# Routed expert stage in pairs of tiles, on one Trainium2 core

## The reference, cut to what matters

```python
ys = _geglu(xf @ Ws1 + bs1) @ Ws2 + bs2                    # shared expert
top_val, top_idx = jax.lax.top_k((xf @ Wr + br) / TAU, 2)
w = ...                                                    # softmax of the two, one-hot over 12
h = jnp.einsum('nd,edh->enh', xf, We1) + be1[:, None, :]   # first layer, 256 -> 2 x 768
yE = jnp.einsum('enh,ehd->end', _geglu(h), We2) + be2[:, None, :]
yr = jnp.einsum('end,ne->nd', yE, w)                       # out = ys + yr + residual
```

## Time and profile before

| | us |
|---|---|
| median of 3 runs (824.36 to 825.64) | 825.05 |
| the profiled execution, its own time | 824.58 |
| its span | 822.7 |
| PE busy | 793.7 |
| DVE busy | 571.9 |
| POOL busy | 406.8 |
| ACT busy | 301.0 |

### The profile page before, as it was taken

The page is one execution under the profiler, slowest core; times in us unless marked ns, Lnnn a source line. Parts: engine busy times, 40 slices in busy tenths (PEclk is TensorE's granted clock), DMA queues, the critical chain, the costliest instruction groups (busy, mean ns, idle before and its releaser), DMA issues. The chain is left out here.

```text
span 822.7 us, 27871 instructions
## 1 busy us (share of the span) xinstructions
PE 793.7 (96%) x9379; PEld 663.5 (81%) x9380; DVE 571.9 (70%) x1323; ACT 301.0 (37%) x855; POOL 406.8 (49%) x511
## 2 busy tenths in 40 slices
PE   8989999999999999889999999999999999999994
PEld 7778888888888888657777888888888888888884
DVE  3887777777777779867886666766766666666652
ACT  1434444444444444443332333333333333333330
POOL 3144444444444444200103477777777777777762
PEclk9999999999999999999999999999999999999998
DMA  8634555555555543026853222322322322322222
GB/s 275 209 106 158 172 167 174 175 175 175 173 151 177 171 121 99 2 70 187 267 194 87 80 38 35 39 34 33 39 35 33 39 35 33 41 33 34 40 29 27
DMA packets 49294, 85.61 MB, mean 104 GB/s; under 512 B 7298, under 2 KB 27970, under 8 KB 49122
## 3 DMA queue, kind: packets, MB, share of 16 engines
q1 hardware_dynamic: 33778, 68.83, 26.2%
q0 software_dynamic: 13888, 15.13, 13.8%
q10 hardware_dynamic: 1584, 1.10, 0.5%
HBM read 68.48 MB, written 16.55 MB: 103 GB/s over the span
## 5 line engine op out<-in xcount | busy, mean ns | idle before, releaser
L1515 PE MATMUL ps<-arena,stage 128*128 x900 | 206.6, 379 | 0.0
L1515 PEld LDWEIGHTS ps<-arena,stage 128*128 128x128 f32 x900 | 165.2, 190 | 19.5
L494 POOL DMA_INDIRECT out_dram<-stage,to_row x75 | 120.7, 1609 | 75.0 <-DVE stage L1098 68.2
L674 ACT ACTIVATE stage<-ps 128x384 f32<-128x384 f32 x150 | 65.4, 488 | 241.1 <-PE ps L1502 241.1
L1502 PE MATMUL ps<-token_rows,token_rows_T 64*128 64x128 f32 x1800 | 129.2, 272 | 0.0
L1502 PEld LDWEIGHTS ps<-token_rows,token_rows_T 64*128 64x128 f32 x1800 | 118.8, 188 | 1.7
L486 POOL DMA_INDIRECT token_rows<-gated_rows,from_row x75 | 75.2, 1003 | 63.9 <-DVE to_row L980 41.2
L1072 DVE COPY token_rows<-ps 128x128 f32<-128x128 f32 x75 | 21.8, 291 | 111.6 <-PE ps L1484 111.6
L401 POOL TENSOR_TENSOR arena<-arena 128x256 f32<-128x256 f32 x32 | 23.4, 731 | 153.4 <-DVE arena L797 140.9
L760 DVE TENSOR_REDUCE arena<-ps 128x8 f32<-128x512 f32 x64 | 43.8, 685 | 65.7 <-PE ps L1224 65.1
L1082 DVE TENSOR_TENSOR stage<-ps,stage 128x384 f32<-128x384 f32 x150 | 75.9, 547 | 1.8 <-ACT stage L674 1.8
(11 more groups left out here) (173 smaller groups left out, 1474.3 us busy)
## 6 DMA issues: line engine op xcount, KB each, us to landing
stage<-in_we_dram SPq DMA_DIRECT2D x36, 512.0 KB, 4.4
arena<-in_cond_w_dram SPq DMA_DIRECT2D x64, 256.0 KB
arena<-in_we_dram SPq DMA_DIRECT2D x12, 768.0 KB, 4.8
arena<-in_x_both_dram SPq DMA_DIRECT2D x31, 256.0 KB, 2.6
arena<-in_L_cond_bias_dram SPq DMA_DIRECT2D x64, 64.0 KB, 3.0
out_dram<-arena SPq DMA_DIRECT2D x32, 128.0 KB, 1.7
be_bc<-in_be_rows_dram SPq DMA_DIRECT2D x13, 192.0 KB, 2.8
gated_rows<-token_rows POOLq DMA_DIRECT2D x2, 1152.0 KB, 11.2
```

The costliest lines, as they stand in the source:

```text
L494: pool.indirect_dma_start(out_rows, bass.IndirectOffsetOnAxis(to_row[:, t:t + 1], 0), y_sb[t % YR], None, compute_op=ALU.add).then_inc(d_a ...
L674: nc.scalar.activation(g_sb[hf].rearrange("p (j n) -> p j n", n=P), first_out[1][:, :, hf, :], ACT.Gelu).then_inc(g_ok, 1)
L1515: last = mm(ps[:, 4 + s % 2, 0:D], actT_sb[s % 2][:, hf, j * P:(j + 1) * P], arena[:, ds(e * E2 + (NJ * hf + j) * D, D)], start=(hf == 0 a ...
```

## The change

The routed stage goes in pairs of tiles. Tile 0 goes alone, and then for each odd t PE does first_layer(t), first_layer(t+1), rows_transpose(t+2), rows_transpose(t+3), second_layer(t-2), second_layer(t-1). The first layer gets two PSUM places (banks 0 to 5, two banks of them shared by both places), the second layer writes to bank 6 or 7, and there are three product buffers, the third in the space of `ws2`. ACT copies the bias weights in place of POOL. ACT widens the rows of tiles t+4 and t+5 at the end of pair t, and POOL issues both gathers and both additions of a pair in a row.

The core of the diff, shortened, in the order POOL, ACT, DVE, PE:

```diff
+            def next_rows(t):
+                pool.wait_ge(y_ok, t + 1)
+                if t + RING < NS:
+                    load_rows(t + RING, t % RING)
+            pool.wait_ge(h_ps, 1)
+            copy_last(2)
+            for t in range(1, NS, 2):
+                for n in (t + 2, t + 3):
+                    if n < NS:
+                        pool.wait_ge(h_ps, n - 1)
+                        copy_last(n)
+                if t > 1:
+                    add_rows(t - 2, (t - 2) % RING)
+                    next_rows(t - 2)
+                    next_rows(t - 1)
+                add_rows(t - 1, (t - 1) % RING)
+                if t == 1:
+                    next_rows(0)
...
+            def gelus(t, s, turn_of=None):
+                act.wait_ge(h_ps, t + 1)
+                if s % 2 == 1:
+                    act.wait_ge(h_first, turn_of)
+                for hf in range(2):
+                    if not isinstance(t, int) or t > 0:
+                        act.wait_ge(act_ok, 2 * t + (hf - 1))
...
+            def tile_weights(t, s):
+                copy_first(act, copy, t, s, 0)
+                e = act.value_load(...)
+                copy(w1bx[s % 2].bitcast(bf16), w1b[:, ds(e * (NJ * P), NJ * P)]).then_inc(w1bx_ok, 1)
+            def two_tiles(t, k, q):
+                for d in range(2):
+                    gelus(t + d, k + d, 3 * q + (k + 1) // 2)
+                    tile_weights(t + d + 2, k + d + 2)
+                for d in (4, 5):
+                    widen(t + d, (k + d) % RING, 16 * q + 16 * ((k + d) // RING) + 16)
...
+            def multiply(t, s):
+                for hf in range(2):
+                    dve.wait_ge(g_ok, 2 * t + (hf + 1))
+                    ...
+                    elif hf == 0:
+                        dve.wait_ge(y_ps, t - 2)
+                    V.tensor_tensor(actT_sb[s % 3][:, hf, :]...)
+            def two_tiles(t, k):
+                multiply(t, k)
+                for d in (2, 3):
+                    rowT_copy(t + d, (k + d) % RING, t + 4)
+                copy_first(dve, V.tensor_copy, t + 2, k, 1)
+                gate_bias(t - 2, (k - 2) % RING)
+                gate_bias(t - 1, (k - 1) % RING)
+                add_bias(t - 2, (k - 2) % RING)
+                multiply(t + 1, k + 1)
+                copy_first(dve, V.tensor_copy, t + 3, k + 1, 1)
+                add_bias(t - 1, (k - 1) % RING)
...
+            def second_layer(t, s):
+                pe.wait_ge(y_ok, ... t - 1)
+                if bank == 7:
+                    pe.wait_ge(rowT_sb, ... t + 5)
+            def two_tiles(t, k):
+                for d in (0, 1):
+                    first_layer(t + d, k + d)
+                for d in (2, 3):
+                    rows_transpose(t + d, (k + d) % RING)
+                for d in (2, 1):
+                    second_layer(t - d, (k - d) % RING)
```

More of the change, by code:

```diff
@@ L691, in _ @@
             for t in range(2):
-                copy_first(act, copy, t, t, 0)
+                tile_weights(t, t)
             shared_gelu(TOK // U - 1)
[L694 to L697, removed]
+            widen(2, 2, 16)
+            gelus(0, 0)
+            tile_weights(2, 2)
+            for t in (3, 4):
+                widen(t, t, 16)
+            for k in (1, 3, 5):
+                two_tiles(k, k, 0)
+            with act.Fori(1, NS // RING - 1) as q:
+                for k in (1, 3, 5):
+                    two_tiles(RING * q + k, k, q)
+            for k in (1, 3, 5):
+                two_tiles(NS - 3 - RING + k, k, NS // RING - 1)
+            two_tiles(NS - 2, 1, NS // RING)
         @block.vector
@@ L1092, in add_bias @@
             def add_bias(t, s):
+                bank = 6 if s % 2 == 1 or isinstance(t, int) and t == 0 else 7
                 dve.wait_ge(y_ps, t + 1)
@@ L1124, in _ @@
                 combine(TOK // U - 2, v, 0)
+            for t in (1, 2):
+                rowT_copy(t, t, 3)
+            multiply(0, 0)
+            copy_first(dve, V.tensor_copy, 2, 2, 1)
+            for v in range(2):
+                combine_last(v)
             dve.wait_ge(d_be2, 16)
-            routed_tiles(0, first=True)
+            for k in (1, 3, 5):
+                two_tiles(k, k)
             with dve.Fori(1, NS // RING) as q:
-                routed_tiles(q)
-            routed_tiles(NS // RING, last=True)
-            add_bias(NS - 1, (NS - 1) % RING)
+                for k in (1, 3, 5):
+                    two_tiles(RING * q + k, k)
+            two_tiles(NS - 2, 1)
+            for t in (NS - 2, NS - 1):
+                gate_bias(t, t % RING)
+            for t in (NS - 2, NS - 1):
+                add_bias(t, t % RING)
         @block.tensor
@@ L1518, in second_layer @@
                 last.then_inc(y_ps, 1)
[L1520 to L1531, removed]
+            def two_tiles(t, k):
+                known = isinstance(t, int)
+                for d in (0, 1):
+                    first_layer(t + d, k + d)
+                for d in (2, 3):
+                    if not (known and t + d >= NS):
+                        rows_transpose(t + d, (k + d) % RING)
+                for d in (2, 1):
+                    if not (known and t < d):
+                        second_layer(t - d, (k - d) % RING)
             rows_transpose(0, 0)
@@ L1535, in _ @@
             first_layer(0, 0)
[L1536 to L1537 removed]
+            for t in (1, 2):
+                rows_transpose(t, t)
+            shared_out(TOK // U - 1, 1, into=last_shared)
             pe.wait_ge(d_w2, 16 * NE)
             pe.wait_ge(r_done, 1)
[L1540 removed]
+            for k in (1, 3, 5):
+                two_tiles(k, k)
             with pe.Fori(1, NS // RING) as q:
[L1542 to L1543 removed]
+                for k in (1, 3, 5):
+                    two_tiles(RING * q + k, k)
+            two_tiles(NS - 2, 1)
+            for t in (NS - 2, NS - 1):
+                second_layer(t, t % RING)
 def shape_constants():
```

135 lines of the change are left out of this document (65 added, 70 removed).

## The result

The changed kernel takes 902.8 us (median of four runs, 898.2 to 907.5) beside 825.2 for the kernel before: a ratio of 1.094, 95% interval 1.087 to 1.102. The profiled execution has a span of 896.8 us. The forecast was 896 us, with a range of 874 to 930.

The account below looks back on a forecast made before the run. PE bounds the kernel before; the change's gather loop was to take 11.4 us per pair against PE's 9.46. Start to 477.6, 34 turns of 387.6, end 28.6: span 893.8, plus 1.9, forecast 896 us, range 874 to 930.

Parts of the forecast that it names:

- The mechanism: Loop from add_bias through scatter, gathers, widening, gelu and DVE to the next add_bias sets the pace: 11.4 us per pair.
- step 1: On POOL, add_rows(t-2) starts 0.29 after add_bias(t-2) and takes 1.61, done at 1.90 us.
- The landing: Second gather's rows are seen 2.8 us after its start, lower bound 2.5; widening then starts at 6.33.
- The register reads: Reads before copy_first and two gate_bias on DVE: taken as 1.2 us together, bounds 0.95 and 1.95.
- steps 5 and 6: DVE after the gelus start: multiply and two rowT_copy until 9.74, then copy_first and two gate_bias until 10.94.
- The sum: One pair to the next takes 11.4 us against PE's 9.46; bounds 10.85 and 12.15; 34 turns give 387.6.
- the clock falls: Rival: PE at half clock needs 18.9 in place of 9.46 us per pair, about 1170 us; chance 0.03.
- Start and end: add_bias(1) done at 477.6; after add_bias(69) at 865.2 another 28.6 us to the end, span 893.8.
- the rival's 0.65 per pair: Rival: POOL's DMAs hold DVE's copy_first, delaying the second gather; 12.05 us per pair, 918 us; chance 0.12.
- That the loop does not bind: Rival: rows arrive in time, PE stays the bound and gains 0.09 at 37 joints, 821.7 us; chance 0.06.

Follow-up runs that it names:

- gathers_first: The changed kernel with POOL issuing both gathers of a pair ahead of the scatter add_rows(t-2): 872.5 us, ratio 1.056.
- fill: The changed kernel with two more 128x256 matmuls per pair on PE, read by nothing, before the second transpose: 891.6 us, ratio 1.081.
- ring12_direct: ring12 with both gathers replaced by plain transfers of 128 neighbouring rows, not the tile's own: 829.5 us, ratio 1.006.
- ring12: The changed kernel with twelve row buffers in place of six, so each gather is issued six tiles earlier: 877.3 us, ratio 1.064.
- before_two_gathers: The kernel before the change with twelve row buffers and gathers two in a row behind every second scatter: 841.0 us, ratio 1.020.
- late_widen: The changed kernel with ACT widening tiles t+2 and t+3 behind the gelus of tile t, not t+4 and t+5 at pair's end: 1037.6 us, ratio 1.257.
- ring12_gathers_last: ring12 with POOL's order scatter, scatter, gather, gather: 847.4 us, ratio 1.028.

## Why the prediction was right, step by step

Times run from the end of add_bias of tile t-2, 650.77 in the timeline above.

| step | predicted | measured |
|---|---|---|
| 1. scatter done on POOL | 1.90 | 1.88 |
| 2. second gather starts | 3.53 | 3.52 |
| 3. its rows are there, widening starts | 6.33 | 6.10 |
| 4. gelus start | 6.83 | 6.61 |
| 5. both rowT_copy done | 9.74 | 9.51 |
| 6. copy and two gate_bias done | 10.94 | 10.58 |
| 7. add_bias done | 11.4 | 11.06 |

**The mechanism** was as forecast, and gathers_first, which takes the scatter of step 1 out of the loop, confirms it. The landing was over-sized by 0.2: it is seen 2.58 after the start, not 2.8. The register reads took 1.07 where I took 1.2, between the two ends of 0.95 and 1.95 and near the lower one. The Trainium skill (Advanced Engine Details and Errata, section Engine Queue Depths) would have hidden them wholly; the row is 0.1 above that. PE's second layer has a new start of its own, 0.5 us ("issue") behind the transposes, that I had not counted. It hides behind VectorE's steps 5 and 6.

**The sum** came out by errors that cancel, and that it came within 7 us is in part luck. The turn in the table takes 11.06, the median one 11.19; with 11.19 the 34 turns are 7 us shorter than forecast. The mean turn takes 11.39, because the clock falls in four of them. The rival "the clock falls" was thus true in a mild form: the stretch 620 to 630 has 0.83, and fill, without the long turns, gave 11 us back. I had set the forecast's clock at 1.00. The Trainium skill's warning (TensorE: Matmul & The Clock Gate, section Loop structure matters more than you think) deserved a price between nothing and 1170 us. The spread of the runs over 9 us goes with it: the two near 907 had a mean clock of 0.97, the others 0.98.

**Start and end.** add_bias(1) was done at 478.94 (predicted 477.6). The scatter of tile 69 starts at 866.39, so its add_bias was done at 866.1, and the end came 30.7 later (predicted 28.6). Both terms are small misses, together 3.4 us. The first is the clock's again: that add_bias waited 1.62 us for the second layer, with a granted clock of 0.83 from 470 to 480.

**The rivals.** POOL's scatters do not hold DVE to their end here: copy_first at 651.62 takes 0.28 while the scatter runs from 651.05 to 652.65. Of 32 such copies that lie wholly inside a scatter (500 to 860 us) 15 take about 0.3 and 17 about 0.6, and the add_bias behind them waits for PE (0.79 at 652.69, 0.63 at 663.94), so the rival's 0.65 per pair is not seen. What makes the difference between 0.3 and 0.6 is not shown. That the loop does not bind was given 821.7. Had it been so, that time was still wrong: in ring12_direct, where it doesn't bind, the pairs are 9.31 apart (additions of tiles 1 and 69 start at 476.48 and 793.04) beside 9.47 before (469.10 and 791.00), 5.3 us gained in 34 turns. But the first starts 7.4 later and the end comes 4.7 later behind tile 69, 829.5 in all. The late end is the scatters': that of tile 69 starts at 799.16, 5.64 after its addition, where it was 0.29 before, and waits for the one before it to land. I had worked out the later start for my forecast and left it out of the rival.

**The large result.** Of the 78 us lost, about 11 are the clock by the medians, 8.5 by the profiled executions of this kernel and of fill. ring12 takes the wait for gathered rows away and gets only 25 back, since held signals take its place; spacing the gathers gives 41 more. In the changed kernel itself held signals cost next to nothing ("remote" waits of 0.7 us at the gelu): while its gathers land, ACT waits for the rows anyway.

## What to carry to other kernels

When an order of work is changed, follow each buffer from its release to its next use through every queue on the way, and compare that loop with the bound engine's work per turn: the times of the timeline's rows gave this one within 0.35 us of the 11.06 measured. When a wait is taken away, expect the next one at nearly the same length, and look whether its releaser was really late. On this evidence it is better not to issue two gathers by index in a row on POOL if a copy that another engine waits for stands behind them; and where PE's signals fall into their time, read the waits of a trace to see if they are held.

## What the runs showed that I had not expected

- With two gathers by index 1.3 us apart, signals that PE sends while they are under way can reach ACT and DVE late: 2.7 to 2.8 us after the first gather's start in before_two_gathers (14 gelus, with rowT_copy beside them), mostly 3.0 to 3.3 after the second one's in late_widen and ring12. It is not so for all: 22 signals of ring12_gathers_last, at times that overlap, came within 0.15. Two plain transfers in a row, or one plain and one by index, showed nothing of it, nor did one gather alone. The semaphores' numbers are not the cause. What the signals share with the gathers, which of them are held, and why the release counts from the first in one kernel and from the second in the others, stays open.
- Two small extra matmuls in PE's pause made a kernel 11 us faster, with the granted clock at 1.00 in place of 0.98.
